# Attention: three fused add, scale and minimum passes in place of three maxima, their combination and the bias

## What is computed

```python
q = _fq_sym(q, axis=-1); k = _fq_sym(k, axis=-1); v = _fq_sym(v, axis=2)   # integers times a step
attn = jnp.einsum('bhqd,bhkd->bhqk', q, k)
attn = jax.nn.softmax(attn.astype(jnp.float32), axis=-1)
attn = _fq_unsigned(attn, axis=-1)      # steps of (largest of the row) / 255
out = jnp.einsum('bhqk,bhkd->bhqd', attn, v)
```

## Time and profile before

| | us |
|---|---|
| median of 3 runs | 2473.56 |
| lowest and highest run | 2473.38 and 2480.1 |
| profiled execution | 2477.05 |
| its span in the trace | 2475.3 |
| TensorE busy (weight loads) | 1950.7 (1265.1) |
| VectorE busy | 1785.8 |
| ScalarE busy | 1634.9 |
| GpSimd busy | 501.7 |

### The profile page before, as it was taken

One profiled execution on the slowest core, in us unless ns is written; L12 is line 12 of the kernel. 1 busy time (PEld: TensorE's weight loads), 2 busy tenths in 40 slices (PEclk: granted clock), 3 DMA queues, 4 the chain that ended last, 5 costly groups with the idle time before them and its releaser, 6 DMA issues. The chain is left out here.

```text
span 2475.3 us, 42289 instructions
## 1 busy us (share of the span) xinstructions
PE 1950.7 (79%) x12019; PEld 1265.1 (51%) x12084; DVE 1785.8 (72%) x2918; ACT 1634.9 (66%) x2564; POOL 501.7 (20%) x410
## 2 busy tenths in 40 slices
PE   5886999999999999995466776767767677773698
PEld 4664878777787877773353222222222222223587
DVE  4996676777767687775646888888888888885333
ACT  3775888888888888881436767677676767772111
POOL 0000555555555555550000000000000000001000
PEclk9997999999999999997876555555555555556799
DMA  1002000000000000001004878778777877881000
GB/s 57 17 8 86 0 26 0 25 0 25 25 0 25 0 25 0 25 0 49 7 0 77 153 146 149 147 148 149 146 148 147 149 148 147 149 155 52 18 17 17
DMA packets 558402, 164.84 MB, mean 67 GB/s; under 512 B 535073, under 2 KB 550817, under 8 KB 558369
## 3 DMA queue, kind: packets, MB, share of 16 engines
q1 hardware_dynamic: 558368, 164.44, 33.4%
HBM read 28.09 MB, written 2.10 MB: 12 GB/s over the span
## 5 line engine op out<-in xcount | busy, mean ns | idle before, releaser
L1222 ACT ACTIVATE levels<-s_ps,nb,qstep 128x1024 int16<-128x1024 f32 x512 | 612.2, 1199 | 267.6 <-DVE nb L1180 267.6
L1170 DVE TENSOR_REDUCE mx<-s_ps 128x1 f32<-128x512 f32 (+1 forms) x768 | 659.5, 865 | 98.3 <-PE s_ps L1115 81.5
L1115 PE MATMUL s_ps<-kT,qT 48*128 48x512 bf16 x1024 | 521.9, 612 | 264.5 <-ACT levels L1222 262.6
L588 DVE SCALAR_TENSOR_TENSOR xs<-x_ps,cw,xs 128x508 f32<-128x508 f32 (+2 forms) x393 | 291.3, 741 | 174.8 <-ACT xs L510 137.4
L1115 PEld LDWEIGHTS s_ps<-kT,qT 48*128 (+1 forms) x1024 | 82.4, 104 | 514.3 <-issue 490.9
L479 PE MATMUL o_ps<-wo,hid 128*128 x1024 | 243.0, 380 | 4.7 <-DVE acc L575 4.7
L644 POOL TENSOR_TENSOR hid<-y,sg 128x512 f32<-128x512 f32 x128 | 175.4, 1370 | 278.6 <-ACT sg L532 185.8
L1125 PEld LDWEIGHTS ao_ps<-vi,levels_T 128*128 128x128 f16 x4096 | 129.5, 105 | 185.2 <-issue 185.2
L1340 POOL TENSOR_TENSOR o_rstd<-o_mv,o_minus_half 128x16 f32<-128x16 f32 x1 | 2.9, 2902 | 1037.7 <-DVE o_mv L902 1037.7
L479 PEld LDWEIGHTS o_ps<-wo,hid 128*128 128x128 f32 x1024 | 192.6, 189 | 40.2 <-issue 9.8
L510 ACT ACTIVATE xs<-x_ps,cb,cw 128x512 f32<-128x512 f32 x131 | 101.9, 778 | 116.9 <-PE x_ps L431 116.9
(11 more groups left out here) (195 smaller groups left out, 3356.3 us busy)
## 6 DMA issues: line engine op xcount, KB each, us to landing
w_raw<-winT_dram SPq DMA_DIRECT2D x18, 512.0 KB, 4.5
wo_raw<-woutT_dram SPq DMA_DIRECT2D x9, 512.0 KB, 5.6
levels_T<-levels SPq DMA_TRANSPOSE x256, 4.3
w_bc<-winT_dram SPq DMA_DIRECT2D x18, 128.0 KB, 2.2
xT<-xT_dram SPq DMA_DIRECT2D x4, 512.0 KB, 7.9
acc<-x_dram SPq DMA_DIRECT2D x1, 2048.0 KB, 11.0
ctxT<-ctxT_dram SPq DMA_DIRECT2D x4, 512.0 KB, 7.5
out_dram<-f_out SPq DMA_DIRECT2D x16, 128.0 KB, 1.7
```

Of the source, the lines that this page charges most:

```text
L588: dve.scalar_tensor_tensor(to, x_ps[:, :, 0:SEQ - s], cw[:, head, TAPS - 1 - s], to, ALU.mult, ALU.add).then_inc(chain if s < TAPS - 1 els ...
L1115: return pe.matmul(s_ps[:, BANKS[h % 2][chunk], :], qT[:, bass.ds(round_, 1), h % NH, :].rearrange("p b t -> p (b t)"), kT[:, h % NH, at:a ...
L1170: dve.tensor_reduce(mx[:, h % 2, at:at + 1], src, AX.XY if what == "cd" else AX.X, ALU.max).then_inc(max_chain, 1)
L1222: act.activation(levels[:, s, half * HALF:(half + 1) * HALF].rearrange("p (c k) -> p c k", c=2), s_ps[:, first:first + 2, :], ACT.Exp, bia ...
```

## The change

`maxima` and `bias` are replaced by `lowest`. It is one instruction a call, `tensor_tensor_reduce`: it computes (score + shift) * nstep for each element, writes it to `spill` (bf16, not read by anybody), and gives the minimum over the elements and a seed. With shift = ln 255 / (-step) and nstep = -step, an element is ln 255 - step * score, so the minimum over all keys is `nb`. The pass over b starts from 3.0e38, that over c and d from the result for b, that over a from the result for c and d; the last one's result is `nb` itself. Each waits for the one before (`low_chain`, and b for `nb_ready`). `shift` and `nstep` hold one round only and are made anew by `steps`, at the last head of a round, by three small dependent instructions. `sums` holds two rounds in place of sixteen (in `finish` and in `exps` its index is `last % 2` and `qt % 2`). TensorE's wait for `consts` goes.

```diff
@@ -1063,19 +1063,20 @@
-        mx = sb("mx", [P, 2, 3])
-        mall = sb("mall", [P, 2])
+        low = sb("low", [P, 2, 2])
         nb = sb("nb", [P, 2])
-        nstep = sb("nstep", [P, BATCH, NH])
+        shift = sb("shift", [P, NH])
+        spill = sb("spill", [P, HALF], BF16)
+        nstep = sb("nstep", [P, NH])
...
-        sums = sb("sums", [P, BATCH, NH, 2])
+        sums = sb("sums", [P, 2, NH, 2])
...
@@ -1146,7 +1147,6 @@
-            pe.wait_ge(consts, 1)
             score(0, 0, "b").then_inc(b_ready, 1)
...
@@ -1160,29 +1160,47 @@
-            def maxima(n, h, what):
...
-                dve.tensor_reduce(mx[:, h % 2, at:at + 1], src, AX.XY if what == "cd" else AX.X,
-                                  ALU.max).then_inc(max_chain, 1)
-
-            def bias(n, qt, h):
-
-                u = h % 2
-                dve.wait_ge(max_chain, n * 4 + 3)
-                dve.scalar_tensor_tensor(mall[:, u:u + 1], mx[:, u, 0:1], mx[:, u, 1:2], mx[:, u, 2:3],
-                                         ALU.max, ALU.max).then_inc(max_chain, 1)
-                dve.wait_ge(max_chain, n * 4 + 4)
-                dve.tensor_scalar(nb[:, u:u + 1], mall[:, u:u + 1], nstep[:, bass.ds(qt, 1), h % NH], LN255,
-                                  ALU.mult, ALU.add).then_inc(nb_ready, 1)
+            def lowest(n, h, what):
+
+                u = h % 2
+                bank = BANKS[u]
+                ready, first, banks, init, to, done = {
+                    "b": (b_ready, bank["b"], 1, 3.0e38, low[:, u, 0:1], low_chain),
+                    "cd": (cd_ready, bank["c"], 2, low[:, u, 0:1], low[:, u, 1:2], low_chain),
+                    "a": (a_ready, bank["a"], 1, low[:, u, 1:2], nb[:, u:u + 1], nb_ready)}[what]
                 dve.wait_ge(ready, n + 1)
+                if what != "b":
+                    dve.sem_inc(held, 1)
+                    dve.wait_ge(low_chain, n * 2 + (1 if what == "cd" else 2))
+                elif not (isinstance(n, int) and n == 0):
+                    dve.sem_inc(held, 1)
+                    dve.wait_ge(nb_ready, n)
+                dve.sem_inc(held, 1)
+                dve.tensor_tensor_reduce(spill[:, 0:banks * GT],
+                                         s_ps[:, first:first + banks, :].rearrange("p c k -> p (c k)"),
+                                         shift[:, h % NH:h % NH + 1].to_broadcast([P, banks * GT]),
+                                         nstep[:, h % NH:h % NH + 1], init,
+                                         ALU.add, ALU.min, to).then_inc(done, 1)
+
+            def steps(at):
+
+                if not (isinstance(at, int) and at == 0):
+                    dve.wait_ge(nb_ready, at * NH)
+                    dve.sem_inc(held, 1)
+                dve.tensor_scalar(nstep[:, :], qstep[:, bass.ds(at, 1), :].rearrange("p q h -> p (q h)"),
+                                  -1.0, None, ALU.mult).then_inc(step_chain, 1)
+                dve.wait_ge(step_chain, at * 3 + 1)
+                dve.sem_inc(held, 1)
+                dve.reciprocal(shift[:, :], nstep[:, :]).then_inc(step_chain, 1)
+                dve.wait_ge(step_chain, at * 3 + 2)
+                dve.sem_inc(held, 1)
+                dve.tensor_scalar(shift[:, :], shift[:, :], LN255, None, ALU.mult).then_inc(step_chain, 1)
+                dve.wait_ge(step_chain, at * 3 + 3)
+                dve.sem_inc(held, 1)
...
@@ -1195,21 +1213,20 @@
             def body(qt):
                 for h in range(NH):
                     n = qt * NH + h
+                    if h == NH - 1 and exists(qt, h, 1):
+                        steps(qt + 1)
                     if exists(qt, h, 1):
-                        maxima(n + 1, h + 1, "b")
+                        lowest(n + 1, h + 1, "b")
                     if h == LAG and exists(qt, 0, -1):
                         finish(qt, qt - 1)
                     if exists(qt, h, 1):
-                        maxima(n + 1, h + 1, "cd")
-                        maxima(n + 1, h + 1, "a")
-                        bias(n + 1, qt if h < NH - 1 else qt + 1, h + 1)
...
+                        lowest(n + 1, h + 1, "cd")
+                        lowest(n + 1, h + 1, "a")
...
```

More of the change, by code:

```diff
@@ L1076, in attention @@
         o_ps = ctx.enter_context(nc.psum_tensor("ao_ps", [P, GT], F32))
-        consts, a_ready, b_ready, cd_ready, max_chain, nb_ready, ab_exp, cd_exp, pv_done, scaled, chain = (
-            sem("at_" + n) for n in ("consts", "a_ready", "b_ready", "cd_ready", "max_chain", "nb_ready", "ab_exp",
+        step_chain, a_ready, b_ready, cd_ready, low_chain, nb_ready, ab_exp, cd_exp, pv_done, scaled, chain = (
+            sem("at_" + n) for n in ("step_chain", "a_ready", "b_ready", "cd_ready", "low_chain", "nb_ready", "ab_exp",
                                      "cd_exp", "pv_done", "scaled", "chain"))
@@ L1162, in _ @@
         def _(dve):
-            def maxima(n, h, what):
[L1165 to L1168, removed]
-                dve.wait_ge(ready, n + 1)
-                dve.tensor_reduce(mx[:, h % 2, at:at + 1], src, AX.XY if what == "cd" else AX.X,
-                                  ALU.max).then_inc(max_chain, 1)
@@ L1183, in finish @@
             def finish(qt, last):
-                both = sums[:, bass.ds(last, 1), :, :].rearrange("p q h s -> p (q h) s")
+                both = sums[:, bass.ds(last % 2, 1), :, :].rearrange("p q h s -> p (q h) s")
                 dve.wait_ge(pv_done, last * NH + NH)
@@ L1202, in body @@
                     if exists(qt, h, 1):
-                        maxima(n + 1, h + 1, "cd")
-                        maxima(n + 1, h + 1, "a")
-                        bias(n + 1, qt if h < NH - 1 else qt + 1, h + 1)
[L1207 to L1212, removed]
+                        lowest(n + 1, h + 1, "cd")
+                        lowest(n + 1, h + 1, "a")
+            steps(0)
+            lowest(0, 0, "b")
+            lowest(0, 0, "cd")
+            lowest(0, 0, "a")
             rounds(dve, body)
@@ L1223, in exps @@
                                ACT.Exp, bias=nb[:, u:u + 1], scale=qstep[:, bass.ds(qt, 1), h],
-                               accum_out=sums[:, bass.ds(qt, 1), h, half:half + 1].rearrange("p q s -> p (q s)")
+                               accum_out=sums[:, bass.ds(qt % 2, 1), h, half:half + 1].rearrange("p q s -> p (q s)")
                                ).then_inc(cd_exp if half else ab_exp, 1)
```

## The result

| | us |
|---|---|
| before, median of 4 runs | 2474.32 |
| after, median of 4 runs | 2507.28 |
| lowest and highest run after | 2506.86 and 2512.36 |
| span of the profiled execution after (before) | 2505.7 (2475.3) |

The ratio is 1.0133, with a 95% interval from 1.0113 to 1.0153: slower by 33 us, where 26 were forecast.

What follows compares the result with a forecast made beforehand. A dependence loop through ScalarE, TensorE and VectorE, 3.495 us a unit, was taken as the bound; 256 times (3.354 + 3x - 3.495) + 15.2 + 5.4, x = 0.054, gave +26 us, so 2500 us; range 2430 to 2575.

Steps and rivals of the forecast that it cites:

- The bound moves to VectorE's series: Attention, each unit: VectorE runs b, cd and a strictly in series, 3.516 us, and becomes the bound.
- the signs that the prediction named: Profile after: no VectorE idling before a; passes near 740, 1350, 820 ns, each with a read; gaps 0.15; scores of a ready.
- Dearer passes: VectorE's three passes: pointer operands and seeds raise their sum to 2.904 us a unit, against 2.597 for the maxima.
- Gaps: VectorE, between passes that wait for each other: three gaps of 0.15 us, 0.45 us a unit.
- The read: VectorE, accumulator read behind each pass: it adds x, taken as 0.054 us, three times a unit.
- the rival of a cheap read: VectorE's accumulator read: x from -0.04 to 0.01, -46 to -8 us, 2428 to 2466 us; chance 0.22.
- steps: VectorE, once a round: three small dependent instructions and three gaps, 1.01 us, times 15 is 15.2 us, not hidden.
- finish: VectorE, once a round: it delays by about 0.80 instead of 0.44 us, 15 times 0.36 is 5.4 us.
- The loop over ScalarE: From exponential through scores of a and pass over a to the next exponential: 3.18 us, shorter than VectorE's series.
- not late: TensorE's scores of c and d: finished 3.94 us after the exponential, wanted by their pass at 4.2.
- Half rate: Rival, VectorE's passes: two cycles an element with an accumulator, +546 us, 3045 us; chance 0.02.
- doing what it removes: Rival: passes cost no more than the maxima, gaps 0.04; -123 us, 2350 us; chance 0.05.

Runs made afterwards that it cites:

- e1_free_b: The changed kernel with the pass over b writing its own buffer, so it no longer waits for the previous unit's pass over a: 2485.32 us, 1.0021 times before.
- e4_two_free: The changed kernel, b writing its own buffer and the pass over c and d seeded by a constant, so only a waits for a pass: 2470.16 us.
- e3_one_held: The changed kernel with one semaphore increment instead of two between the waits and each pass: 2501.01 us in one run.
- e2_steps_once: The changed kernel with nstep and shift made once, for the first round, and used in all later rounds: 2482.87 us, 1.0017 times before.
- e5_no_mall: The kernel before without combining the three maxima; nb is made from chunk a's maximum alone: 2413.92 us in one run.

## Why the prediction was right, step by step

- **The bound moves to VectorE's series.** Right. VectorE's wait for the scores fell from 81.5 to 0.4 us, and e1_free_b, which takes one wait (with its increment) out of the series and leaves the work as it is, made the kernel 21 us faster. All the signs that the prediction named came, but for the size of the gaps.
- **Dearer passes.** 0.738, 1.348 and 0.818 were forecast; 0.751, 1.344 and 0.810 were measured, a sum of 2.905 against 2.904. The pointer rows carried over to an operation that the trace of before did not show. The second pointer costs 0.06 rather than 0.08 (e4_two_free, and 810 against 751), the first pass 0.013 more than forecast; these two small errors cancel in the sum.
- **Gaps.** 0.19 us, not 0.15: mis-sized by 3 x 0.04 = 0.12 us a unit, 31 us over 256 units. The earlier trace rows held for ordinary instructions: the reciprocal and the last instruction of `steps` follow 0.15 us behind their predecessors (1442.62 + 0.25 to 1443.02). e3_one_held shows that the earlier increment is not the reason for the 0.04 more. That the fused pass itself starts more slowly is what is left, but no run shows it alone.
- **The read.** x was 0.054; measured, the read starts 0.07 us before the pass's recorded end and lasts 0.083, so x is about 0.01: mis-sized by 3 x 0.04 the other way. I had taken an instruction of 0.154 us and an overlap of 0.10, of which the earlier trace rows give only 0.08 for VectorE (`nb`, 1704.56 + 0.21 to 1704.69); it is 0.083 and 0.07. The two errors, gaps and read, cancel, and the period of 3.516 came out at 3.496. Had only one of them been made, the period's term would have been off by 31 us. That the period was nearly right is thus partly luck; the read by itself fell at the edge of the range I had given to the rival of a cheap read, and the kernel was slower all the same, because the gaps and `steps` took its gain. "VectorE: DVE Perf Modes" of the Trainium skill, in "Two Vector instructions with no wait between them", says that an operation with an accumulator output is a main instruction and a read; this trace agrees, with 83 ns for the read.
- **What a wait costs.** "VectorE: DVE Perf Modes" of the Trainium skill says in "The DRAIN you can't avoid" that a semaphore after each of several chained copies costs nothing extra. Here b followed a after 1.00 us with the wait (1704.49 to 1705.49 in the kernel after), and after 0.74 without it (1701.91 to 1702.65 in e1_free_b). The page's copies were not run here. The measurement decides for this kernel: a wait between fused passes, with the increment beside it, cost 0.26 us.
- **steps.** 1.01 us a round was forecast, 1.44 measured (e2_steps_once): 15.2 against 21.6 us. The three instructions take 0.17, 0.25 and 0.18, two of them longer than the 128x1 row that I took; the gap behind the last is 0.48 and not 0.15 (1443.02 + 0.18 to 1443.68). Two further waits with their increments stand there; that these make the difference is argued from the code.
- **finish.** 15 x 0.36 = 5.4 us forecast; (7.717 - 2 x 3.496) - (7.429 - 2 x 3.509) = 0.31 a round, 4.7 us. Right.
- **The sum, term by term.** From first to last unit 28.3 us were measured; the sum gave 26. The 3.495 was a mean over all intervals of the kernel before, the two faster rounds outside the loop included, so it gives the right total for before, though an ordinary unit inside the loop takes 3.509. The errors lie in the kernel after: the period, 3.496 for 3.516, is -5.1 us over 255 intervals; `steps` is +6.4; `finish` delays VectorE by 0.725 (7.717 - 2 x 3.496) and not 0.80, -1.1; and each round's end takes 0.14 us more than two ordinary units even without `steps` (7.13 on the mean of all 15 in e2_steps_once, less 2 x 3.496), which was not in the sum, +2.1. That makes 28.3. The medians differ by 33; 2 us of the rest lie ahead of attention in the profiled executions, and the others are within the spread of the runs.
- **The loop over ScalarE** at 3.18 us was too low, by 0.20 (e4_two_free). This did not harm the forecast, since 3.38 is still under 3.49, but it put my expectations for e1_free_b and e4_two_free wrong. So did the scores of c and d, "not late" at 4.2 against 3.94. Both figures were too small. With the 1.41 us of e1_free_b the pass can come 4.32 us after the exponential (2.91 to the start of the scores, and 1.41), and in the kernel after it comes at 4.47 (3.49, and 1701.97 to 1702.95). "Not late" was right, with 0.15 us to spare, and in e1_free_b it no longer was.
- **Rivals.** Half rate did not come: 1344 ns for 1024 elements. The change "doing what it removes" did not come either: the passes cost 0.31 us a unit more than the maxima and the gaps were 0.19, not 0.04. Its figure of 2350 was not tested. e5_no_mall, without `mall` and with the cheap maxima, took 2414, but it keeps `nb`.

## What to carry to other kernels

A fusion that takes small steps off one engine's loop can tie its instructions to each other: count the new same-engine waits at their full gap, because here three gaps of 0.19 us and 0.31 us of dearer operands made a series as long as the loop from which the small steps had gone. Ask of each added wait whether it protects data or only a scratch buffer; a separate scratch for one pass took a wait away at once (e1_free_b). Work out the second and third longest loop too, with the same care as the longest: here they lay 0.1 us below it, and it took four small edits (scratch, order of waits, order of TensorE, place of `finish`) and one copy a round to turn 1.0133 into 0.9881.

## What I had not expected

A unit of the kernel before takes 3.29 us in the rounds outside the loop and 3.50 inside. The timeline of the first round of the kernel before, in the columns of the earlier trace rows:

```profile
1334.89 0.22 DVE L1177 SCALAR_TENSOR_TENSOR mall<-mx 128x1 f32<-128x1 f32 x1
1335.14 0.21 DVE L1180 TENSOR_SCALAR nb<-mall,nstep 128x1 f32<-128x1 f32 x1
...
1335.39 1.20 ACT L1222 ACTIVATE levels<-s_ps,nb,qstep 128x1024 int16<-128x1024 f32 x1 [0.81 <-DVE nb L1180]
```

Between `mall`'s end and `nb` are 0.03 us, and from `nb`'s start to the exponential 0.25; inside the loop it is 0.13 and 0.36. Inside the loop both instructions take operands whose address comes from the round's register (`nstep` and `qstep`), and a register instruction stands between the wait and the instruction. That this is the cause is argued from the code and these rows, and the record bears it out only in part. For it: in the kernel after, whose passes take their operands from fixed places, the gaps are 0.19 and the unit 3.50 inside the loop and outside. Against it, for ScalarE: e2_steps_once took the round's register out of the scale of the exponentials, and one unit inside its loop reads

```profile
1705.45 0.09 DVE L1179 DVE_READ_ACCUMULATOR2_ANT nb<- 128x1 f32 x1
1705.66 1.20 ACT L1237 ACTIVATE levels<-s_ps,nb,qstep 128x1024 int16<-128x1024 f32 x1 [1.01 <-DVE nb L1179]
```

From the end of `nb`'s read to the exponential are 0.12 to 0.13 us in most units of that loop, against 0.15 to 0.16 in the kernel after and 0.04 in the first round of both. So the scale's address accounts for some 0.03 of the 0.12 us; what the other 0.09 are stays open (the place in `sums` and the wait's count still come from registers). If all of it could be taken away, it would be worth 0.2 us a unit on the kernel before, 47 us in all; this is an estimate from 0.21 us and the 224 units inside the loop.
